# A four-layer graph kernel: q and its pairs in two buffers each, two adjacency pieces at other places, and some of ScalarE's score rows made by VectorE

## What is computed

```python
# layers 0, 2, 3: a graph convolution with a normalized adjacency
d = sum(adj [+ eye, abs], axis=-1) ** -0.5
out = (d[:, :, None] * adj * d[:, None, :]) @ x @ W + b
# layer 1: additive attention
q, k = x @ WQ, x @ WK
score[i, j] = sum_d p[d] * relu(q[j, d] + k[i, d])      # 2048 x 2048 x 128 in every batch
out = softmax(score + (0 where adj > 0, else -1e22)) @ x
```

## Time and profile before

| | us |
|---|---|
| median of 3 runs | 14031.23 (14029.29 to 14034.36) |
| the profiled execution | 14031.93 |
| its span, first to last instruction | 14030.1 |
| TensorE busy | 13002.6 (93%) |
| VectorE busy | 13269.3 (95%) |
| ScalarE busy | 13100.1 (93%) |
| GpSimd busy | 1060.3 (8%) |
| mean granted TensorE clock | 0.982 of full speed |

### The profile page before, as it was taken

One profiled execution on the slowest core, in us unless ns is written; L12 is line 12 of the kernel. 1 busy time (PEld: TensorE's weight loads), 2 busy tenths in 40 slices (PEclk: granted clock), 3 DMA queues, 4 the chain that ended last, 5 costly groups with the idle time before them and its releaser, 6 DMA issues. The chain is left out here.

```text
span 14030.1 us, 318060 instructions
## 1 busy us (share of the span) xinstructions
PE 13002.6 (93%) x143877; PEld 5489.3 (39%) x143877; DVE 13269.3 (95%) x13964; ACT 13100.1 (93%) x8612; POOL 1060.3 (8%) x699
## 2 busy tenths in 40 slices
PE   7889989999899998999989999999989999899988
PEld 3333434444344433444334443344433444333333
DVE  6999999999999999999999999999999999999995
ACT  5999999999999999999999999999999999999994
POOL 0000000010000100001000100001000010000000
PEclk8999999999999999999999999999999999999999
DMA  5111112221122111221122211222112221011103
GB/s 187 46 51 47 49 53 83 86 66 51 55 85 90 61 43 62 88 88 58 39 72 86 86 58 40 72 83 87 58 36 75 90 80 58 30 50 52 43 12 109
DMA packets 714332, 935.48 MB, mean 67 GB/s; under 512 B 61712, under 2 KB 455952, under 8 KB 693520
## 3 DMA queue, kind: packets, MB, share of 16 engines
q1 hardware_dynamic: 712976, 915.13, 20.9%
HBM read 722.01 MB, written 184.55 MB: 65 GB/s over the span
## 5 line engine op out<-in xcount | busy, mean ns | idle before, releaser
L1055 DVE TENSOR_SCALAR big<-q_pair,k_pair_cols 128x2048 f32<-128x2048 f32 x10036 | 12122.4, 1283 | 426.5 <-PE score L1203 409.1
L815 ACT ACTIVATE big<-q_f,k_cols 128x2048 f32<-128x2048 f32 x6144 | 11792.8, 1998 | 320.5 <-PE score L1203 275.3
L1203 PE MATMUL score<-big,unit_window 128*32 128x512 f16 x81920 | 5181.7, 396 | 708.5 <-DVE big L1055 674.3
L1203 PE MATMUL score<-big,sign_window 128*32 128x512 f32 x49152 | 5626.6, 598 | 194.9 <-ACT big L815 191.6
L1203 PEld LDWEIGHTS score<-big,unit_window 128*32 128x32 bf16 x81920 | 2292.5, 96 | 3850.2 <-issue 1070.0
L1203 PEld LDWEIGHTS score<-big,sign_window 128*32 128x32 f32 x49152 | 1577.2, 111 | 3520.0 <-issue 3009.7
L1122 PE MATMUL acc<-piece,gs 128*128 128x512 f32 x3072 | 1442.7, 597 | 36.8 <-DVE gs L913 22.4
L625 POOL TENSOR_SCALAR att_var<-att_mom 128x1 f32<-128x1 f32 x128 | 63.8, 498 | 10048.3 <-DVE att_mom L1020 10048.3
L1122 PEld LDWEIGHTS acc<-piece,gs 128*128 128x128 f32 x3072 | 532.7, 191 | 544.7 <-issue 457.8
L1181 PE MATMUL acc<-x,att_turned 128*128 128x128 f32 x4096 | 555.0, 279 | 0.0
L1181 PEld LDWEIGHTS acc<-x,att_turned 128*128 128x128 f32 x4096 | 498.4, 192 | 56.8 <-issue 56.8
(11 more groups left out here) (90 smaller groups left out, 2757.0 us busy)
## 6 DMA issues: line engine op xcount, KB each, us to landing
piece<-adj_turned SPq DMA_DIRECT2D x1536, 256.0 KB, 2.8
att<-in_adj_dram SPq DMA_DIRECT2D x128, 1024.0 KB, 5.2
raw<-in_adj_dram SPq DMA_DIRECT2D x224, 512.0 KB, 4.8
adj_turned<-turned SPq DMA_DIRECT2D x224, 512.0 KB, 5.0
big<-in_adj_dram SPq DMA_DIRECT2D x32, 512.0 KB, 7.5
adj_turned<-big SPq DMA_DIRECT2D x32, 512.0 KB, 6.9
gx<-in_x_dram SPq DMA_DIRECT2D x32, 256.0 KB, 3.9
q_kept<-raw SPq DMA_DIRECT2D x32, 256.0 KB, 3.8
```

What stands on the lines that cost most here:

```text
L815: ins = nc.scalar.activation(ring["A"][:, RANK[g] % RING * 4 + u, :], q_f32[:], ACT.Relu, bias=k_cols[:, t % 2, QUAD * u + g:QUAD * u + g ...
L1055: ins = nc.vector.tensor_scalar(ring["D"][:, RANK[g] % RING * 4 + u, :], q_pair[:], k_pair_cols[:, t % 2, QUAD * u + g:QUAD * u + g + 1], ...
L1203: ins = nc.tensor.matmul(score[QUAD * u:QUAD * (u + 1), cc, :], window[:, QUAD - 1 - g:2 * QUAD - 1 - g], row, start=(g == 0 and part == 0 ...
```

## The change

- **Two buffers each for q and its pairs**, `q_bufs` and `pair_bufs`, swapped by batch. The buffer that attention doesn't use in a batch holds what `gs` (now `scaled(c)`, in q's) and `raw` and `turned` (now `raw(c)` and `stage(c)`, in the pairs') held. q and its pairs of the next batch are loaded at t 15, group 21, behind the load of k. The first raw load of a batch waits for the last rows of VectorE and POOL of the batch before, and VectorE's scaling for layer2 for ScalarE's last rows of the batch before.
- **The mask** is added after row (1, 0) at t 0 too, and POOL makes its row of group 1 also at t 0, except in the very first block.
- **Two pieces**, 6 and 7, move from group 6 to groups 1 and 4, on TensorE and, with the loads that follow them, on SyncE.
- **Lent rows**: in blocks in which a unit's first slot lies (t 0 to 8, not in LAST), VectorE makes row 3 of ScalarE's group 18, and, if the block has no layer step, also row 3 of group 7. Such a row is in pair form, so TensorE multiplies it as two f16 halves within a group of which the other three rows are f32.

```diff
-    PIECES_AT = {-4: [0, 1, 2], 0: [3, 4, 5], 6: [6, 7], 10: [8, 9], 14: [10], 18: [11], 23: [12, 13, 14, 15]}
+    PIECES_AT = {-4: [0, 1, 2], 0: [3, 4, 5], 1: [6], 4: [7], 10: [8, 9], 14: [10], 18: [11], 23: [12, 13, 14, 15]}
...
-        q_f32 = sb("q_f32", [P, N])
-        q_pair = sb("q_pair", [P, N])
+        q_bufs = [sb(f"q_f32_{i}", [P, N]) for i in range(2)]
+        pair_bufs = [sb(f"q_pair_{i}", [P, N]) for i in range(2)]
...
+        def q_of(b):
+            return q_bufs[b % 2][:]
+        def pairs_of(b):
+            return pair_bufs[b % 2][:]
+        def scaled(c):
+            return q_bufs[c % 2][:].rearrange("p (t f) -> p t f", f=D)
+        def raw(c):
+            return pair_bufs[c % 2][:, 0:HALF]
+        def stage(c):
+            return pair_bufs[c % 2][:, HALF:N]
...
         def masked_at(t):
-            return (0, 0) if t == 0 else (1, 1)
+            return (1, 1)
...
         def has_pool_row(c, t):
-            return t > 0
+            return t > 0 or not one_of(c, FIRST)
...
+        LENT_ROWS = [(18, 3), (7, 3)]
+
+        def lent_rows(c, t):
+            if not units_where(c, lambda u: slot_place(2 * u) // GROUPS == t):
+                return []
+            return LENT_ROWS[:1 if steps_at(c, t * GROUPS + SELF_AT, SELF_AT) else 2]
...
                     sp.wait_ge(pair_stored, split_of(c + 1, STEPS, 0) * 16)
+                    if not one_of(c, FIRST):
+                        sp.wait_ge(rows_ready["D"], (c + 1) * (T * N_OF["D"]))
+                        sp.wait_ge(pool_row_ready, pool_rows(c, 0))
+                        sp.wait_ge(pool_sum_row_ready, sum_rows(c, 0))
...
             def load_q(c):
                 sp.wait_ge(q_stored, qk_step(c + 1, STEPS) * 16)
+                sp.wait_ge(piece_used, piece_of(c - 1, "layer0", STEPS - 1, T, AHEAD))
+                sp.dma_start(q_of(c + 1), q_kept[c + 1]).then_inc(q_loaded, 16)
+                sp.wait_ge(k_stored, qk_step(c + 1, STEPS) * 16)
                 sp.wait_ge(pair_stored, split_of(c + 1, STEPS, 0) * 16)
-                if not one_of(c, FIRST):
-                    sp.wait_ge(rows_ready["A"], (c + 1) * (T * N_OF["A"]))
-                sp.dma_start(q_f32[:], q_kept[c + 1]).then_inc(q_loaded, 16)
-                if not one_of(c, FIRST):
-                    sp.wait_ge(rows_ready["D"], (c + 1) * (T * N_OF["D"]))
-                    sp.wait_ge(pool_row_ready, pool_rows(c, 0))
-                    sp.wait_ge(pool_sum_row_ready, sum_rows(c, 0))
-                sp.dma_start(q_pair[:], q_pair_kept[c + 1]).then_inc(q_pair_loaded, 16)
+                sp.dma_start(pairs_of(c + 1), q_pair_kept[c + 1]).then_inc(q_pair_loaded, 16)
...
                         elif not one_of(c, LAST):
                             load_k(c + 1, 0)
+                            load_q(c + 1)
...
-                if not one_of(c, LAST):
-                    load_q(c + 1)
...
+                            if (g, u) in lent_rows(c, t):
+                                continue
...
+                if name == "layer2":
+                    dve.wait_ge(rows_ready["A"], (c + 1) * (T * N_OF["A"]))
...
+                    for h, u in lent_rows(c, t):
+                        if h == g:
+                            dve.wait_ge(rows_used["A"], n * N_OF["A"] + (RANK[g] + 1))
+                            nc.vector.tensor_scalar(ring["A"][:, RANK[g] % RING * 4 + u, :], pairs_of(c + 1),
+                                                    k_pair_cols[:, t % 2, QUAD * u + g:QUAD * u + g + 1],
+                                                    None, ALU.max).then_inc(lent_row_ready, 1)
...
-                window = unit_window if kind == "D" else sign_window
+                lent = [u for h, u in lent_rows(c, t) if h == g]
+                if lent:
+                    pe.wait_ge(lent_row_ready, lent_before(c, t, g) + 1)
                 for cc in range(CHUNKS):
...
-                    for part in range(2 if kind == "D" else 1):
+                    for part in range(2 if kind == "D" or lent else 1):
                         for u in range(P // QUAD):
+                            pair = kind == "D" or u in lent
+                            if part == 1 and not pair:
+                                continue
                             row = ring[kind][:, RANK[g] % RING * 4 + u, :]
-                            row = halves(row)[:, cc * BANK:(cc + 1) * BANK, part] if kind == "D" else \
+                            row = halves(row)[:, cc * BANK:(cc + 1) * BANK, part] if pair else \
                                 row[:, cc * BANK:(cc + 1) * BANK]
```

More of the change, by code:

```diff
@@ L111, in build, with x1_turned, q_new, high @@
         bias = {n: sb("bias_" + n, [P, P]) for n in ("layer0", "layer2", "layer3")}
-        w_raw, squares = gs[:, 0, :], gs[:, 2:4, :]
+        def q_of(b):
[8 more added lines that the diff above has]
+            return pair_bufs[c % 2][:, HALF:N]
+        def x1_turned(c):
+            return raw(c)[:, 0:BANK]
+        def q_new(c):
+            return raw(c)[:, BANK:2 * BANK]
+        k_new = x1_turned
+        def high(c):
+            return stage(c)[:, 0:BANK]
+        def pair_new(c):
+            return stage(c)[:, BANK:2 * BANK]
+        w_raw, squares = scaled(0)[:, 0, :], scaled(0)[:, 2:4, :]
         p_col = sb("p_col", [P, 1])
@@ L259, in sum_rows, with lent_before @@
             return sum(has_sum_row(a, k) for a in range(FIRST, c + 1) for k in range(T) if a < c or k < t)
+        LENT_ROWS = [(18, 3), (7, 3)]
[3 more added lines that the diff above has]
+            return LENT_ROWS[:1 if steps_at(c, t * GROUPS + SELF_AT, SELF_AT) else 2]
+        def lent_before(c, t, g):
+            return sum(len(lent_rows(a, k)) for a in range(FIRST, c + 1) for k in range(T) if a < c or k < t) + \
+                sum(h < g for h, _ in lent_rows(c, t))
         OPENING, FIRST, LAST, CLOSING = -2, -1, B - 2, B - 1
@@ L418, in load_raw @@
                     sp.wait_ge(raw_abs_summed, unit_of(b, u))
-                sp.dma_start(raw[:], half_rows(b, u)).then_inc(raw_loaded, 16)
+                sp.dma_start(raw(c), half_rows(b, u)).then_inc(raw_loaded, 16)
             def load_piece(c, name, s, i):
@@ L968, in split @@
                     dve.wait_ge(pair_stored, split_of(b, s, i) * 16)
-                low = halves(pair_new)[:, :, 0]
-                nc.vector.tensor_tensor(low, (src, high)[i], (high, src)[i], ALU.subtract).then_inc(low_written, 1)
+                low = halves(pair_new(c))[:, :, 0]
+                nc.vector.tensor_tensor(low, (src, high(c))[i], (high(c), src)[i], ALU.subtract).then_inc(low_written, 1)
             def side(c, place):
@@ L1121, in add_piece @@
                            (s * (T // PIECES) + i // PIECES + 1) * 16)
-                nc.tensor.matmul(acc[1][:], gs[:, i, :], piece[:, i % PIECES, :], start=(i == 0), stop=(i == T - 1)) \
+                nc.tensor.matmul(acc[1][:], scaled(c)[:, i, :], piece[:, i % PIECES, :], start=(i == 0), stop=(i == T - 1)) \
                     .then_inc(piece_used, 1)
@@ L1127, in add_self @@
                 for j in range(PER):
-                    nc.tensor.matmul(acc[1][:, j * P:(j + 1) * P], gs[:, s * PER + j, :], ident[:], start=False, stop=False)
+                    nc.tensor.matmul(acc[1][:, j * P:(j + 1) * P], scaled(c)[:, s * PER + j, :], ident[:], start=False, stop=False)
             def project(c, name, s):
@@ L1151, in queries_keys @@
                         pe.wait_ge(turn_free[1], turn_use(c, (name, s)) + AHEAD)
-                        nc.tensor.matmul(turn[1][:], w_sb[name][:], x1_turned, start=True, stop=True) \
+                        nc.tensor.matmul(turn[1][:], w_sb[name][:], x1_turned(c), start=True, stop=True) \
                             .then_inc(turn_full[1], 1)
```

58 lines of the change are left out of this document (26 added, 32 removed).

## The result

| | before | after |
|---|---|---|
| median, us | 14032.11 (4 runs, 14029.29 to 14034.36) | 13918.78 (4 runs, 13915.48 to 13924.0) |
| profiled execution, us | 14031.93 | 13915.48 |
| its span, us | 14030.1 | 13913.6 |
| mean granted clock | 0.982 | 0.987 |

What follows compares the result with a forecast made beforehand. No engine bounds throughout: ScalarE paces raw-tile blocks without a layer step, VectorE blocks with neither; step blocks have neither full alone. From 14031.93 us, -18 - 37 - 11 - 10 = -76 gives about 13955; own range 13,900 to 13,990, bounds 13800 to 14025.

Steps and rivals of the forecast that it cites:

- First batch, lent rows, -18: Blocks t 0 to 8 of the first batch: 18 rows go from ScalarE to VectorE, 931.5 against 949.1 us.
- Batch changes, -37: Blocks t 15, 0 and 1: six changes at -5.3 us, in all -32, and the last at -5.
- Lent rows in step blocks, -11: Blocks t 2 to 8: TensorE no longer waits for ScalarE late in a block, 1.8 us a batch, six times.
- VectorE pays its row out of 4 to 6 us of idle time: Blocks t 2 to 8: VectorE's idle time was to cover the lent row of 1.208 us.
- What a mixed group costs, 0: Groups with one lent f16 row beside three f32 rows: still 3.43 us from start to start, 0 taken.
- Moving pieces gives nothing by itself: Pieces 6 and 7 into the gap before group 4: the gap moves to group 9, block length stays, 0.
- The clock, -10: 84 step blocks: fewer falls to 1.2 GHz after group 4's gap, some at group 9; -73 to +53, net -10.
- From group 9 on TensorE is continuous with the same work.: Step blocks: VectorE's rows bind group 9; behind it TensorE runs on without pause, so moving work gives 0.
- that the gap before group 4 takes work (13795): Rival, 17%: VectorE uses its idle time in step blocks, each 1.9 us shorter, 160 us less, 13795.
- That the clock falls after the moved gap in every step block: Rival, 10%: the gap before group 9 drops TensorE's clock in all 84 blocks, +63 us on the sum, 14018.
- That the batch ends stay: Rival, 8%: the raw load or the mask holds VectorE as q did, the 37 us stay, 13992.
- That mixed groups are slow: Rival, 12%: 42 lent groups in step blocks cost +1.8 us each (14031, no change) or +3.4 (14098, slower).

## Why the prediction came out as it did, step by step

The sign, the places and the order of the terms were right, and 13918.78 lies inside both ranges. The sum was 37 us too small. Two errors of opposite sign stand in the step blocks (lent rows 22 us too good, clock some 35 too bad), and that they partly cancel is luck; most of the rest is at the batch changes.

- *First batch, lent rows, -18.* Measured -21.1, and the run with lent rows alone has -20.4 of it. VectorE's idle time is 10.9 us (forecast near 11).
- *Batch changes, -37.* Right mechanism, too small: -60.7, and -9.7 in the change shown instead of -5.3. Two terms of the sum were mis-sized and one was put at nothing. I gave VectorE 3.6 us idle in the three blocks and it has 311.30 - 309.63 = 1.7; and I put its busy time at 308.5 + 3.6 = 312.1, where it is 309.6. The last change, without lent rows, has 0.9 us idle (1.8 assumed) and 303.1 busy (304.6 assumed). The row for the floor, 0.55 us, stood in the earlier trace rows; why the busy time came out lower is not shown. The term at nothing is the clock: the sum had it in step blocks only, but t 15 had two falls in each of the seven batches, and moving the pieces alone gained 13.5 us at the changes (8.0 beside the two buffers). That ScalarE's 4.88 us would go as well was half right, 2.64 stay.
- *Lent rows in step blocks, -11.* The wait that they were to remove, before group 26, is removed (-0.33 us a block). What failed is "VectorE pays its row out of 4 to 6 us of idle time": it has that time, but not ahead of group 20, where its rows already came just in time in 18 of 42 blocks and now do so in all of them (+0.50 us a block). With 0.09 before group 30 the term is +11, not -11.
- *What a mixed group costs, 0.* Right: the three f32 strips keep their pace and group 19 ends as before. The rivals at +1.8 and +3.4 are out. The Trainium skill's rule in "TensorE: Matmul & The Clock Gate", section "What overlaps and what doesn't", that matmuls start and end strictly in program order, doesn't describe these records across column strips: f16 instructions of one strip run beside the f32 ones of the other three, and one of group 19 starts at 5778.86, before f32 ones of group 18 at 5779.20 and 5779.62 that stand ahead of it in the program.
- *Moving pieces gives nothing by itself.* Right: a t 4 at full clock lasts 106.9 us with the pieces moved and 106.7 without. The gap went from group 4 to group 9, as forecast (0.43 and 1.71 us, forecast 0.6 and 2).
- *The clock, -10.* Right sign, wrong size. Of the 84 step blocks 49 had the fall at group 4 (forecast 56), and in the changed kernel none has. 13 have one around group 9, where I had allowed 42. By my prices that is 49 x 1.3 - 13 x 1.5 = 44 us. The step blocks of the run with the pieces alone gained 37; in the changed kernel it is 34.4 with the lent rows' 11 already paid.
- *"From group 9 on TensorE is continuous with the same work."* Incomplete. It holds in blocks without raw tiles, where filling the gap before group 9 shortened each by about 1 us. In blocks with raw tiles ScalarE's chain (turn, copy, rows of group 13) ends almost as late, and TensorE's work could only be taken out when the copy had been moved too.

Of the rivals, that the gap before group 4 takes work (13795) is refuted by the pieces alone. That the clock falls after the moved gap in every step block is refuted by 13 falls in 84 blocks. That the batch ends stay is refuted by the earlier trace rows against their counterpart above. That mixed groups are slow is refuted by the timeline of groups 18 to 21. What stays open: why t 15 has fewer falls with the pieces moved, and why VectorE's busy time at the batch changes is below the sum.

## What to carry to other kernels

When three engines are linked by rings of two groups, a visible gap may be only the last of several limits of nearly the same lateness. Here VectorE's rows at group 9 and ScalarE's copy ahead of group 13 stood within 1 to 2 us of each other; in blocks with both, taking work out of the gap gave nothing (+7.7 us) until the copy was moved as well (-39.5), and lent rows that were worth nothing before that were worth 29 us after it. Idle time of an engine in a whole block doesn't say that it can take on work at a given place: VectorE had 4 to 6 us, and one row of 1.2 us still came out as 0.5 us of waiting, because it stood ahead of rows that were just in time. An in-order DMA queue belongs into every move of a consumer: leave the loads behind it where they are, unless what is queued after them can wait. And a fill that moves a gap without shortening the block can still pay, by where TensorE's clock falls; that must be counted block by block, not assumed.

## What the runs showed of the hardware

- In step blocks the gap before group 4 (2.29 and 2.60 us in the earlier trace rows) was followed by a fall to 1.2 GHz in 49 of 84; the one before group 9 that took its place (1.71 us in the block shown) in 13 of 84. With pieces 8 and 9 and the copy moved too, none of the 84 has a fall in either place. The time at the low level after the first score matmul is 393 us before, 231 in the changed kernel and 196 in that one.
- f32 and f16 matmuls in different column strips of one group run side by side, each strip at its own pace: the last matmul of the group behind starts 5.06 us after the first of the mixed group, as it does behind an all-f32 one, and in the lent strip that next group starts before the mixed one has ended in the others (5778.86 against 5779.62).
